# Two delta rules: 64-token blocks in 64 columns, two to a TensorE diagonal, with unrolled loops

## The reference

```
v   = x @ W_write.T,   beta = sigmoid(...)
M   = tril(-(beta*k) @ k.T * exp(cum_i - cum_j), -1)
A   = inverse(I - M)                      # 64 x 64, unit lower triangular
o   = tril((q @ k.T) * exp(cum_i - cum_j), -1) @ (A @ (beta*v))
x   = x + o @ W_read.T
```

```
S = S*exp(g_t);  u = beta_t*(v_t - k_t @ S);  S = S + outer(k_t, u);  o_t = q_t @ S
```

## Time and profile before

| | us |
|---|---|
| median of 3 runs | 3275.9 (3279.45, 3272.79, 3275.9) |
| span of the profiled execution | 3280.8 |
| loop of the first rule | 1132.6 to 1235.8 |
| loop of the second rule | 2688.8 to 3019.7 |
| TensorE busy | 2995.6 (91%) |
| VectorE busy | 2095.6 (64%) |
| ScalarE busy | 1525.3 (46%) |
| GpSimd busy | 1962.2 (60%) |

### The profile page before, as it was taken

One profiled execution on the slowest core, in us unless ns is written; L12 is line 12 of the kernel. 1 busy time (PEld: TensorE's weight loads), 2 busy tenths in 40 slices (PEclk: granted clock), 3 DMA queues, 4 the chain that ended last, 5 costly groups with the idle time before them and its releaser, 6 DMA issues. The chain is left out here.

```text
span 3280.8 us, 62016 instructions
## 1 busy us (share of the span) xinstructions
PE 2995.6 (91%) x19885; PEld 1775.7 (54%) x19932; DVE 2095.6 (64%) x4576; ACT 1525.3 (46%) x2430; POOL 1962.2 (60%) x1263
## 2 busy tenths in 40 slices
PE   5699999999999788997899999999999969998789
PEld 2355555555555586774344444444444438887456
DVE  6477777777777553114767676767677357776653
ACT  2466666666666322335444444444444342222633
POOL 4478778787787330002688888888888714644500
PEclk7799999999999898998999999999999979999789
DMA  6755555555454001001000000000000000000300
GB/s 176 178 169 190 190 176 192 178 185 197 168 192 147 3 1 52 0 0 56 11 30 20 30 20 30 20 30 20 30 20 20 1 9 1 0 0 1 80 4 10
DMA packets 148210, 232.47 MB, mean 71 GB/s; under 512 B 16787, under 2 KB 85851, under 8 KB 148124
## 3 DMA queue, kind: packets, MB, share of 16 engines
q1 hardware_dynamic: 147836, 231.23, 22.1%
q10 hardware_dynamic: 288, 0.13, 0.0%
HBM read 147.80 MB, written 83.52 MB: 71 GB/s over the span
## 5 line engine op out<-in xcount | busy, mean ns | idle before, releaser
L445 POOL TENSOR_TENSOR sb_a_acc<-sb_a_acc,sb_a_PT 128x1024 f32<-128x1024 f32 x252 | 596.7, 2368 | 45.8 <-ACT sb_a_PT L523 39.5
L607 DVE TENSOR_REDUCE sb_a_mx<-ps_a_A 128x1 f32<-128x512 f32 x768 | 506.5, 686 | 107.0 <-PE ps_a_A L771 101.9
L523 ACT ACTIVATE sb_a_PT<-ps_a_SC 128x1024 f32<-128x1024 f32 (+1 forms) x416 | 426.2, 1024 | 298.1 <-PE ps_a_SC L794 268.5
L1703 POOL TENSOR_TENSOR sb_a_acc<-sb_a_acc,sb_a_PT 128x512 f32<-128x512 f32 (+2 forms) x384 | 487.5, 1270 | 37.6 <-ACT sb_a_PT L1799 11.0
L1799 ACT ACTIVATE sb_a_PT<-ps_a_SC 128x1024 f32<-128x1024 f32 (+2 forms) x256 | 234.6, 917 | 563.3 <-PE ps_a_SC L2078 329.9
L2097 PE MATMUL ps_a_PV<-sb_a_PT,sb_a_XN 128*128 128x512 f32 (+2 forms) x896 | 434.9, 602 | 2.2 <-ACT sb_a_PT L1799 0.7
L1892 DVE TENSOR_REDUCE sb_a_mx<-ps_a_A 128x1 f32<-128x512 f32 x384 | 256.8, 679 | 281.0 <-PE ps_a_A L2053 240.0
L2078 PE MATMUL ps_a_SC<-sb_a_QX,sb_a_XT 128*128 128x512 f32 (+1 forms) x832 | 396.7, 596 | 0.1
L771 PE MATMUL ps_a_A<-sb_a_KS,sb_a_QS 97*128 97x512 bf16 x768 | 301.6, 393 | 13.9 <-DVE sb_a_QS L599 7.5
L794 PE MATMUL ps_a_SC<-sb_a_QS,sb_a_KS 105*128 105x128 bf16 (+1 forms) x3328 | 256.8, 220 | 13.4 <-DVE sb_a_QS L621 13.4
L805 PE MATMUL ps_a_PV<-sb_a_PT,sb_a_V 128*32 128x256 f32 (+1 forms) x3328 | 266.6, 392 | 0.4 <-issue 0.3
(11 more groups left out here) (534 smaller groups left out, 5877.7 us busy)
## 6 DMA issues: line engine op xcount, KB each, us to landing
sb_a_C<-in_ctx_dram SPq DMA_DIRECT2D x64, 768.0 KB
a_KD<-sb_a_K SPq DMA_DIRECT2D x192, 256.0 KB, 4.2
sb_a_KS<-a_KD SPq DMA_DIRECT2D x256, 192.0 KB
a_KD<-sb_a_K SPq DMA_DIRECT2D x192, 144.2 KB, 2.7
sb_a_KS<-a_KD SPq DMA_DIRECT2D x256, 108.2 KB
sb_a_QP<-a_QD SPq DMA_DIRECT2D x6, 384.0 KB, 16.6
sb_a_dn<-n_L_ffn_expert_down_dram SPq DMA_DIRECT2D x1, 2048.0 KB, 15.3
a_QD<-sb_a_PT SPq DMA_DIRECT2D x3, 384.0 KB, 6.0
```

The source lines that it names most:

```text
L445: pool.tensor_tensor(acc[:, :], first[:, :], PT[slot(a, j)][:, :], ALU.add).then_inc(s["acc"], 1)
L523: act.activation(PT[slot(a, j)][0:n, :], SC[(a + j) % 2][0:n, :], ACT.Exp).then_inc(s["exp"], 1)
L607: v.tensor_reduce(mx[:, p, c:c + 1], A[u % 2][:, :], AXX, ALU.max).then_inc(s["am"], 1)
L1703: pool.tensor_tensor(acc[a][0:m, :], first, PT[u % 4][0:m, HQ * i:HQ * i + HQ], ALU.add).then_inc(s["acc"], 1)
```

## The change

1. Matrices of `Core` are kept as [128, 4, 64] and not [128, 4, 128]: the two 64x64 blocks of a unit lie one above the other, without the zero quarters. Every product of two such matrices becomes two 64x64 ones, on rows and columns 0 to 63 and 64 to 127 of TensorE. Their results go to the same columns of one bank, in partitions 0 to 63 and 64 to 127. Sums move 256 columns, and operations on VectorE, ScalarE and GpSimd that work on these matrices handle half the elements.
2. The products of keys are made for each half apart, with 64 columns of weights (all 128 rows).
3. The loops are unrolled, and the copies to loop buffers go; the operands are read in place. The turning of a unit's matrix (L964) becomes a product with two stacked identities (`eye2`).
4. In `delta0` W_write and W_read are multiplied once, V is made with the product, and QL times ug is the result: L1209 and L1319 go.
5. `core_consts` makes each mask in two halves of 64 partitions.

```diff
@@ Core @@
-        self.E = two("E", [P, 4, P])
...
-        self.XX = two("XX", [P, 2, 4, P])
-        self.T1s = two("T1s", [P, 4, P])
+    HALVES = (slice(0, T), slice(T, P))
+        self.E = two("E", [P, 4, T])
...
+        self.XX = two("XX", [P, 2, 4, T])
+        self.T1s = two("T1s", [P, 4, T])
...
+        self.T1 = [t[:, 0:2, :].rearrange("p a (b t) -> p (a b) t", t=T) for t in self.T1w]
+        self.PP = [t[:, :, 0:2, :].rearrange("p w a (b t) -> p w (a b) t", t=T) for t in self.PPw]
...
@@ solve @@
             for u in range(4):
-                mm = pe.transpose(self.PP[a][:, 0, u, :], self.Em[a][0][:, u, :], k.ident[:, :])
+                for r in self.HALVES:
+                    mm = pe.matmul(self.PP[a][r, 0, u, :], self.Em[a][0][r, u, :], k.eye2[r, :], start=True, stop=True)
...
                 for u in range(4):
-                    mm = pe.matmul(self.T1[a][:, u, :], self.Em[a][l % 2][:, u, :], self.XX[a][:, 0, u, :], start=True, stop=True)
+                    for r in self.HALVES:
+                        mm = pe.matmul(self.T1[a][r, u, :], self.Em[a][l % 2][r, u, :], self.XX[a][r, 0, u, :], start=True, stop=True)
...
                     if l < LEVELS - 1:
-                        pe.matmul(self.PP[a][:, 0, u, :], self.XX[a][:, 1, u, :], self.T1s[a][:, u, :], start=True, stop=True)
-                    mm = pe.matmul(self.PP[a][:, 1, u, :], self.T1s[a][:, u, :], self.XX[a][:, 1, u, :], start=True, stop=True)
+                        for r in self.HALVES:
+                            pe.matmul(self.PP[a][r, 0, u, :], self.XX[a][r, 1, u, :], self.T1s[a][r, u, :], start=True, stop=True)
+                    for r in self.HALVES:
+                        mm = pe.matmul(self.PP[a][r, 1, u, :], self.T1s[a][r, u, :], self.XX[a][r, 1, u, :], start=True, stop=True)
@@ delta0 @@
-            act.wait_ge(s["wk"], 2 * NG)
-            act.wait_ge(s["vc"], NG)
-            with act.Fori(0, NG // 2) as i:
-                gs = [(a, 2 * i + a) for a in range(2)]
-                for a, g in gs:
-                    wait(act, s["y"], g - 1)
-                    act.activation(wr[a][:, :, :, :].rearrange("p w j t -> p w (j t)"), WR[:, :, bass.ds(g * 512, 512)], ACT.Copy).then_inc(s["cp"], 1)
+            for i in range(NG // 2):
                 core.decays(act, s, i)
-                for a, g in gs:
-                    wait(act, s["u"], g - 1)
-                    act.activation(vg[a][:, :, :], V[:, bass.ds(4 * g, 4), :], ACT.Copy).then_inc(s["cv"], 1)
                 core.copies(act, s, i)
-                for a, g in gs:
-                    wait(act, s["oq"], g + 1)
-                    act.activation(oqs[a][:, :, :], core.W[a][:, :, :], ACT.Copy).then_inc(s["oqs"], 1)
...
-            for i in range(2):
-                mm = pe.transpose(Sm[:, P * i:P * i + P], W[:, i, :], k.ident[:, :])
-            mm.then_inc(s["wt"], 1)
+            pe.transpose(Sm[:, 0:D], W[:, 1, :], k.ident[:, :]).then_inc(s["wt"], 1)
+            pe.wait_ge(s["wc"], 1)
+            pe.matmul(Sm[:, D:2 * D], W[:, 0, :], WRT[:, :], start=True, stop=True).then_inc(s["wt"], 1)
...
-                    mm = pe.matmul(PP[:, c % 2, j, :], k.hT[:, P * n:P * n + P], WT[:, 0, :], start=True, stop=True)
+                    mm = pe.matmul(PP[:, c % 2, j, :], k.hT[:, P * n:P * n + P], WW[:, :], start=True, stop=True)
...
                     for j in range(4):
-                        mm = pe.matmul(core.W[a][:, j, :], ug[a][:, j, :], core.QL[a][:, j, :], start=True, stop=True)
-                    mm.then_inc(s["oq"], 1)
-                for a, g in gs:
-                    wait(pe, s["oqs"], g + 1)
-                    for j in range(4):
-                        mm = pe.matmul(core.PP[a][:, 0, j, :], oqs[a][:, j, :], WT[:, 1, :], start=True, stop=True)
+                        for r in core.HALVES:
+                            mm = pe.matmul(core.W[a][r, j, :], core.QL[a][r, j, :], ug[a][r, j, :], start=True, stop=True)
                     mm.then_inc(s["y"], 1)
@@ delta1 @@
                     for w in range(2):
-                        mm = pe.matmul(core.PP[a][:, w, :, :], kqT[a][:, 0, :], X4[a][:, w, :, :], start=True, stop=True)
+                        for r in core.HALVES:
+                            mm = pe.matmul(core.PP[a][r, w, :, :], kqT[a][:, 0, r], X4[a][:, w, :, r], start=True, stop=True)
...
                     for h in range(H):
-                        mm = pe.matmul(core.W[a][:, h, 0:DV], core.XX[a][:, 1, h, :], vg[a][:, h, :], start=True, stop=True)
+                        for r in core.HALVES:
+                            mm = pe.matmul(core.W[a][r, h, 0:DV], core.XX[a][r, 1, h, :], PR[r, g, VO + DV * h:VO + DV * h + DV], start=True, stop=True)
...
-            with pe.Fori(0, NT // 2 - 1) as i:
-                pair(i, True)
-            pair(NT // 2 - 1, False)
+            for i in range(NT // 2):
+                pair(i, i + 1 < NT // 2)
@@ core_consts @@
+    def both(out, in_, **how):
+
+        for r in Core.HALVES:
+            done(pool.affine_select(out=out[r], in_=in_[r], **how))

```

More of the change, by code:

```diff
@@ L942, in decays @@
             wait(act, s["cum"], 2 * i + a + 1)
[L943 removed]
+            act.activation(self.LT[a][:, :, :], self.T1[a], ACT.Exp).then_inc(s["lt"], 1)
     def copies(self, act, s, i, lo=1, hi=LEVELS):
@@ L1083, in core_consts @@
         done(pool.memset(v4[:, :, 0, :], 0.0))
[L1085 to L1088, removed]
+        both(v4, v4, compare_op=ALU.is_ge, fill=0.0, base=0, pattern=[[-2 * b, T // (2 * b)], [0, 2], [0, b]], channel_multiplier=1)
+        both(v4, v4, compare_op=ALU.is_ge, fill=0.0, base=b - 1, pattern=[[2 * b, T // (2 * b)], [0, 2], [0, b]], channel_multiplier=-1)
 def softplus_vector(v, sem, y, w, p, out):
@@ L1116, in delta0_sems @@
                                        "g3", "g4", "mz")}
-    for n in CORE_SEMS + ("cp", "cv", "oq", "oqs", "y", "lb", "w4", "xa", "x1a"):
+    for n in CORE_SEMS + ("y", "w4", "xa", "x1a"):
         s[n] = k.counted("a1_" + n)
@@ L1145, in stage_delta0 @@
     two = lambda n, sh: [sb(f"{n}{a}", sh) for a in range(2)]
-    wr, ldg, beg = two("wr", [P, 2, 4, P]), two("ldg", [P, 4]), two("beg", [P, 4])
-    ug, vg, oqs = two("ug", [P, 4, D]), two("vg", [P, 4, D]), two("oqs", [P, 4, P])
+    ug = two("ug", [P, 4, D])
     core = Core(k, "a1c", ctx, True)
     flat = lambda t: t[:, :, :].rearrange("p a b -> p (a b)")
-    Gp, Qp = core.PP[0][:, 0], core.PP[0][:, 1]
-    turned = (core.T1[0], core.W[0], core.T1[1], core.W[1])
+    Gp, Qp = core.PPw[0][:, 0], core.PPw[0][:, 1]
+    turned = (core.T1w[0], core.W[0], core.T1w[1], core.W[1])
     by_batch = lambda t, w: t[:, w, :].rearrange("p (b t) -> p b t", t=T)
-    PP, Sm = core.PP[1], flat(core.W[1])
+    PP, Sm = core.PPw[1], flat(core.W[1])
     with nc.Block() as block:
@@ L1293, in _ @@
             pe.wait_ge(s["wk"], 2 * NG)
-            with pe.Fori(0, NG // 2) as i:
+            for i in range(NG // 2):
                 gs = [(a, 2 * i + a) for a in range(2)]
@@ L2206, in stage_delta1 @@
     two = lambda n, sh: [sb(f"{n}{a}", sh) for a in range(2)]
-    kq, kqT = two("kq", [P, 2, P]), two("kqT", [P, 2, P])
+    kqT = two("kqT", [P, 2, P])
     X4 = two("X4", [P, 2, H, P])
-    vg, ug = two("vg", [P, H, DV]), two("ug", [P, H, DV])
-    ldg, beg, ben = two("ldg", [P, H]), two("beg", [P, H]), two("ben", [P, H])
+    ug = two("ug", [P, H, DV])
     OA = ZPf[:, 0:NT * VD].rearrange("p (n c) -> p n c", c=VD)
@@ L2423, in ahead @@
             def ahead(i):
-                for a in range(2):
-                    v.tensor_copy(ldg[a][:, :], ld[:, bass.ds(2 * i + a, 1), :].rearrange("p o h -> p (o h)")).then_inc(s["ll"], 1)
-                    v.tensor_copy(ben[a][:, :], beta[:, bass.ds(2 * i + a, 1), :].rearrange("p o h -> p (o h)")).then_inc(s["ll"], 1)
-                wait(v, s["ll"], 4 * i + 4)
-                core.strengths(v, s, i, [t[:, :] for t in ben])
+                core.strengths(v, s, i, [beta[:, 2 * i + a, :] for a in range(2)])
             def spread(i):
-                core.spread(v, s, i, [t[:, :] for t in ldg])
+                core.spread(v, s, i, [ld[:, 2 * i + a, :] for a in range(2)])
             def pair(i, more):
@@ L2442, in pair @@
                     front(i + 1)
-                core.levels(v, s, i, 3, 4)
-                for a, g in gs:
-                    v.tensor_copy(beg[a][:, :], beta[:, bass.ds(g, 1), :].rearrange("p o h -> p (o h)")).then_inc(s["lb"], 1)
-                core.levels(v, s, i, 4, 5)
+                core.levels(v, s, i, 3, 5)
                 if more:
@@ L2462, in _ @@
             core.gates(v, s, 0)
-            with v.Fori(0, NT // 2 - 1) as i:
-                pair(i, True)
-            pair(NT // 2 - 1, False)
+            for i in range(NT // 2):
+                pair(i, i + 1 < NT // 2)
             wait(v, s["oc"], NT)
@@ L2583, in pair @@
                     for h in range(H):
```

(3 more changed lines are left out.)

124 lines of the change are left out of this document (58 added, 66 removed).

## The result

The changed kernel takes 3107.4 us (median of 4 runs, 3106.7 to 3108.1) against 3277.7 for the one before (median of 4 runs; the three that were known at the forecast gave 3275.9): a ratio of 0.948, with a 95% interval of 0.946 to 0.949. It is 170 us faster; 150 were forecast, and the forecast of 3126 lay 19 too high, inside its range of 3090 to 3215.

What follows compares the result with a forecast made beforehand. TensorE's issue was taken as the bound. Savings of 125 us (second rule) and 46 (first), less 18 for clock and 3 for switching and code, took the 3280.8 span to 3131; the median, 5 lower, gave 3126, range 3090 to 3215.

Steps and rivals of the forecast that it cites:

- TensorE's issue sets the pace: Second rule's pair: TensorE busy 37.34 of 39.9 us; 5.3 of a 6 us level cycle is its issue.
- 0.027 us a record, because quadrants run side by side: Solve's 64x64 products: 0.027 us per record against 0.111 now, narrower and overlapping on two quadrants; forecast 62%.
- the first rival: Solve's products: quadrants run one after another, 0.055 us a record, level cycle 5.5, kernel 3207 us; chance 27%.
- Level cycle 3.2, X4 on the path for 1.8: Second rule's levels: 3.2 us each; VectorE's 3.57 us X4 build between levels 2 and 3 adds 1.8; together 14.7.
- The rest of the pair: Second rule's pair outside the four level steps: 16.0 us now, about 8.9 after, taken as 9.0.
- The taps slow the spread by 1.2: Second rule: in about half the pairs the spread beside GpSimd's taps is late by 1.2 us.
- a forecast of 24.3: Second rule: average pair of 24.3 us, from 23.7 plus late spreads, against 39.9 now; eight pairs save 125.
- The first rule, 57.0 us and 3 for the clock: First rule's loop: 57.0 us against 103.2, 46 saved, with 3 given back for a lower clock.
- The clock, 18 us given back: Both loops: a fifth of the time at 1.2 GHz costs 15 us over eight pairs and 3 in the first rule.
- 87%: near the top, not at it: Second rule's pair: TensorE would show 21 us busy of 24.3, 87%, so the clock is not quite full.
- Masks' setup hidden: Setup at 49 to 65 us: 24 half selects on GpSimd, at most 8.5 us more, covered by a 9.7 us wait.
- Code for the unrolled loops: Unrolled loops: 3 us lost to switching tile shapes and fetching code, no row for it, range 0 to 10.

Runs made afterwards that it cites:

- the reordered kernel: Changed kernel with the solve's products (turns, T1, both PP) issued quadrant by quadrant, rows 0 to 63 of a group, then 64 to 127; 3175.4 us.
- the experiment's expectation: Kernel before with W_write and W_read multiplied once, loops and 128x128 products kept, expected to save 3 to 4 us; 3273.8 against 3279.3, ratio 0.998.
- the unaltered kernel: Changed kernel run again with no edit, as the measure for its variants; 3108.3 us beside the split X4, 3106.6 beside the cut taps.

## Why the prediction was right

- **TensorE's issue sets the pace.** Right: with its issue halved the pair fell from 39.9 to 23.9, and with the same products in a slower order it rose to 29.8. Unrolling alone changed nothing.
- **0.027 us a record, because quadrants run side by side.** Right in kind, and shown by the reordered kernel. The size is 0.029 alternating, 0.055 to 0.06 in one quadrant. The Trainium skill's rule ("TensorEngine Tiling (Array Packing)", Restrictions and Gotchas), read as forbidding two row tiles in one bank whatever their partitions, would have made the first rival; the trace does not agree with that reading. The 16 records of a T1 group write one bank, go to the two quadrants in turn, and follow each other by 0.031 us, where one quadrant alone takes 0.055 to 0.06. With partitions 0 to 63 and 64 to 127 apart, the rule does not bind here. (The rows of the reordered kernel, L973 beside L983 and L984, write different banks and do not test it.)
- **Level cycle 3.2, X4 on the path for 1.8.** Measured 3.28 and 3.26 for the plain steps, 4.00 and 4.08 for the other two. X4 costs 0.8 on the path and not 1.8: it took 3.03 us and not 3.57, and the rest is room that VectorE had in the level over the 1.8 allowed; the turn of the keys, which the forecast had beside other work, costs the other 0.7. Sum 14.6 for 14.7, two errors that cancel. The rest of the pair 9.3 for 9.0.
- **The taps slow the spread by 1.2.** Near in size, and the wrong operation. The two steps of 25.5 are those that begin beside gates of 3.24 us, which the forecast did not name; the step before them has the same slow spread (2.49) with gates of 0.86 and takes 24.1, against 23.9 without taps. So the spread costs about 0.2 on the path and the gates 1.4. The mean of the seven steps between kq products, the first at a low clock, is 24.6 (2646.69 to 2818.88) for a forecast of 24.3.
- **The first rule, 57.0 us and 3 for the clock.** 60.8. The weights' part was 5.6 in the kernel before and not the 3 to 4 of the experiment's expectation; the whole came out to a microsecond, and its parts were not measured one by one.
- **The clock, 18 us given back.** This is the term that was mis-sized. "87%: near the top, not at it" was the step; the profile shows 88 to 92% busy in a pair and a clock of 1.00, and only the start of each loop is below (0.97 and 0.98 over the loops). Taking it out makes the forecast 3108, against 3107.4; so close is partly luck, since the parts above were off both ways. The step fails twice: with an operation added, two pairs at 80% busy kept the full clock as well. The risk was there all the same: in the five pairs beside the taps it fell to 0.84 to 0.89.
- **Masks' setup hidden.** On GpSimd's lines the 24 half selects take 10.4 us, the 12 whole ones took 8.4, and the next work there still waits 9.7 for ScalarE:

```profile
L1078 POOL TENSOR_SCALAR_AFFINE_SELECT sb_LV<-sb_LV 64x64 f32<-64x64 f32 x24 | 10.4, 434 | 1.6
L435 POOL TENSOR_TENSOR sb_a_K<-sb_a_RK,sb_a_K 128x512 bf16<-128x512 f32 (+1 forms) x4 | 3.7, 944 | 9.7 <-ACT sb_a_K L502 9.7
```

(These two from the second run of the unaltered kernel.)

- **Code for the unrolled loops.** The instruction queue went from 49 packets to 88; all waits that the profile lists for TensorE in pairs 1 to 6 are for VectorE. No run shows this term by itself. If it and the switches of tile shape are all of the 0.3 us by which the rest of a pair was longer than forecast, they make some 2 us over all pairs; 3 were allowed.

## What to carry to other kernels

Where a block-diagonal matrix of two 64x64 blocks fills the array with zeros, keep the blocks one above the other and issue two quadrant products next to each other in the queue: it halves TensorE's issue, and the elements of every copy and subtraction as well. Work out the new cycle from group to group with the pipeline's latency, then look for the in-order pieces that used to lie in its gaps; here X4, the turn of the keys and the gates beside GpSimd came onto the path, and cutting up X4 and the taps gave another 9 us. Before giving time back to the clock, work out the share of TensorE's work in the new cycle, and do not count on the share alone: here, with TensorE busy 88 to 92% of a pair, all pairs but the first kept the full clock, and at 80% some did and some did not.

## What the runs showed of the hardware that was not expected

- TensorE's queue reaches past products that wait for their own quadrant: L983 and L984, which come later in the program, started in the upper quadrant between the last L973 of the lower one. With all of a group in one order the record came to 0.047 us instead of 0.058.
- VectorE's operation on two SBUF operands can be held up for much of a GpSimd tap of 4.5 to 5.8 us: 2.98 us for 256 elements (0.41 alone), 3.95 for 512 (0.69), while subtractions that read PSUM, run beside the same taps, kept their 0.69.
- At the same busy share of 80% the granted clock was 0.89 in a pair beside the taps (24.95 of 31.3 us) and 1.00 in one without (22.09 of 27.5), in one run.
